# Group statistics of image 1 partly by a quadratic form: the last four chunks are multiplied out after the statistics are known

## Chip, cores and metric

The kernel runs on one core of a Trainium2 chip. The metric is the time of one execution on the device in microseconds; lower is better. The time before is the median of three runs.

## The reference

Two layers on x of shape (2, 1024, 64, 64), all in fp32. The first is a bottleneck with a deformable 3x3 convolution; its result x1 is the input of the second, a non-local block with a Taylor kernel and a normalisation over the whole image. What matters here is the end of the second:

```
t = einsum('oc,bchw->bohw', Wt, x1)          # and p, g alike, 512 channels
att_k = a_k^2 * sum(p**k * g)                # k = 0, 1, 2, over channels and pixels
y = att_0 + att_1 * t + att_2 * t**2
z = einsum('oc,bchw->bohw', Wz, y)           # 1024 channels
...
out = (z - mean(z)) / sqrt(var(z) + eps) * gn_w + gn_b + x1
```

Mean and variance are taken over all 1024 x 4096 values of an image (`_L1_conv_ref` has one group).

## The kernel before

The order of work on each engine is written out by hand, with semaphores between engines. An image is cut in 8 chunks of 512 pixels, 16 in all (`ALLC`). First the deformable convolution, x1 and the projections t, p, g are made chunk by chunk; x1 and t go to DRAM, the sums of p and g become three coefficients per image (`coefficients`).

Then comes the part that the change is about, a loop over 16 chunks with 8 output tiles each (`KIN` = 8; a tile is 128 channels x 512 pixels), 128 tiles in all, 64 (`ZT`) per image. Images, chunks and tiles are counted from 0: chunk 11 has tiles 88 to 95. For a chunk:

- POOL issues the load of t into `TB` (1 MB), once the low parts of the chunk before it are made.
- y is made in place in four parts (`KCP`): ACT scales (`y_scale`, L907, to two buffers `UB`), DVE multiplies (`y_square`, L1324), ACT rounds to the high part (`y_high`, L919), DVE takes the rest as the low part (`y_low`, L1328). y of chunk c + 1 is made between the tiles of chunk c.
- PE multiplies each tile with Wz in three passes (high x high, high x low, low x high; `product`, L194 to L196), 12 matmuls of 512 columns per tile. The first two and the last two tiles of a chunk are done together (`z_pair`). Six PSUM banks (`ZB`) take turns.
- ACT evicts the tile to one of 71 SBUF buffers (`z_evict`, L972) and DVE takes its statistics (`stats`, L1371). From tile 71 on an eviction waits until the store of the tile 71 before has landed.

When the 64 tiles of an image are in SBUF, the statistics are put together over partitions with two small matmuls (L1622, L1626), and each tile is finished: DVE adds x1 to the scaled tile (`add_x1`, L1406), ACT adds the bias (`fin`, L980), SP stores it. For image 0 this lies between the tiles of image 1, by a rule that says how many adds are through after x tiles of image 1:

```
def adds_by(x):
    return max(0, min(64, max(x - 3, 3 * (x - 5) // 2)))
```

x1 for it comes through four buffers (`XS`, 256 KB each): on SP a load, which waits for the add that frees its buffer, and a store, which waits for its bias pass, take turns. For image 1 it lies behind the last product. Its x1 comes in pairs of tiles (512 KB) into `XT`, slots in memory that is free by then.

## Time and profile before

| | |
|---|---|
| median of 3 runs | 2363.9 us (2363.74 to 2366.23) |
| profiled execution, its own time | 2355.59 us |
| its span | 2353.8 us |
| busy: PE, DVE, ACT, POOL | 2243.0, 1572.7, 1252.0, 778.6 us |
| DMA moved | 667.97 MB, mean 284 GB/s |

The profile is of one execution. Its span runs from the first to the last instruction that it records; the execution's own time is a little longer. PE is the matrix engine (PEld its weight loads), DVE the vector engine, ACT the scalar engine, POOL is GpSimd, SP only issues DMAs. "idle before us <-releaser" says how long an engine stood before an instruction and what ended this. A busy share is an average; here what matters is the last fifth of the span.

### The profile page before, as it was taken

What the parts mean: (1) busy time and instruction counts of PE and PEld (TensorE: products, weight loads), DVE (VectorE), ACT (ScalarE), POOL (GpSimd) and SP (SyncE); (2) the same over time, 40 slices, a digit from 0 to 9 for tenths busy, and PEclk for the clock granted to TensorE, in tenths of its full rate; (3) what the DMA queues carried; (4) which work ended last, traced back from release to release, by engine and by line L of the source; (5) the groups of instructions that cost most, each with busy time, mean ns of one, the idle gap of its engine ahead of it and who ended that gap; (6) DMA issues with size and microseconds to landing.
All of it is one profiled execution on the core that took longest, in us unless ns stands there. A gap on an engine that the chain in (4) does not pass through costs nothing.

```text
span 2353.8 us, 29804 instructions
## 1 busy us (share of the span) xinstructions
PE 2243.0 (95%) x10252; PEld 1853.8 (79%) x10252; DVE 1572.7 (67%) x3177; ACT 1252.0 (53%) x2432; POOL 778.6 (33%) x706
## 2 busy tenths in 40 slices
PE   8999999999989999999999999999999999999970
PEld 6888888888868788888878888788788878887750
DVE  4212325766788898889878988789785324557855
ACT  6444444444465666556655665565553324446745
POOL 0100003333224565556556765666561000000000
PEclk9999999999989999999999999999999999999985
DMA  8988989999998998889889988898884111118979
GB/s 304 320 310 279 314 291 381 403 400 394 401 375 286 315 341 308 297 320 336 288 294 315 314 313 307 295 313 305 289 305 156 60 49 53 54 50 288 314 229 388
DMA packets 289824, 667.97 MB, mean 284 GB/s; under 512 B 27112, under 2 KB 101608, under 8 KB 283528
## 3 DMA queue, kind: packets, MB, share of 16 engines
q0 software_dynamic: 88048, 322.81, 39.4%
q1 hardware_dynamic: 172536, 262.59, 31.4%
q10 hardware_dynamic: 29088, 80.67, 9.4%
q8 instruction: 81, 1.33, 0.2%
q14 instruction: 71, 0.58, 0.1%
HBM read 435.47 MB, written 230.49 MB: 283 GB/s over the span
## 4 chain that ended last, share of the span: by engine, by line
PE 86%; DMA 5%; DVE 5%; SPq 1%; issue 1%; ACT 1%; POOL 0%; ACTq 0%; DVEq 0%
PE bank L194 22%; PE bank L196 22%; PE bank L195 22%; PE bank L1462 5%; PE bank L1463 5%; PE bank L1464 5%; DVE z L1406 2%; PE bank L1480 2%; DMA xs<-x 2%; DMA g<-vwide,tbl 1%; DMA out<-z 1%; PE bank L1488 1%; PE bank L1504 1%; DMA xt<-x 0%; DVE zst L1371 0%
## 5 line engine op out<-in xcount | busy, mean ns | idle before, releaser
L647 POOL DMA_INDIRECT g<-vwide,tbl x512 | 589.9, 1152 | 548.9 <-DVE a L1018 208.1
L194 PE MATMUL bank<-x1h,wlh 128*128 128x512 f32 x1536 | 604.2, 393 | 5.4 <-DVE x1l L1296 3.9
L196 PE MATMUL bank<-x1h,wll 128*128 128x512 f32 x1536 | 601.6, 392 | 2.5 <-issue 2.5
L195 PE MATMUL bank<-x1l,wlh 128*128 128x512 f32 x1536 | 600.6, 391 | 2.8 <-issue 2.7
L1034 DVE SCALAR_TENSOR_TENSOR a<-g,tbl,a 128x256 f32<-128x256 f32 x1224 | 528.8, 479 | 23.7 <-DMA g<-vwide,tbl 18.4
L674 ACT ACTIVATE g<-g,tbl 128x256 f32<-128x256 f32 x1008 | 426.4, 499 | 200.2 <-DMA g<-vwide,tbl 158.1
L194 PEld LDWEIGHTS bank<-x1h,wlh 128*128 128x128 f32 x1536 | 289.4, 188 | 66.5 <-issue 6.1
L196 PEld LDWEIGHTS bank<-x1h,wll 128*128 128x128 f32 x1536 | 289.1, 188 | 66.8 <-issue 4.6
L195 PEld LDWEIGHTS bank<-x1l,wlh 128*128 128x128 f32 x1536 | 289.6, 189 | 66.0 <-issue 5.4
L752 ACT ACTIVATE vb<-bank 128x512 f32<-128x512 f32 (+1 forms) x320 | 174.3, 554 | 195.3 <-PE bank L1464 150.7
L1462 PE MATMUL bank<-w2h,o1h 128*128 128x512 f32 (+1 forms) x640 | 236.7, 370 | 0.0
L1463 PE MATMUL bank<-w2l,o1h 128*128 128x512 f32 (+1 forms) x640 | 235.8, 368 | 0.0
L1464 PE MATMUL bank<-w2h,o1l 128*128 128x512 f32 (+1 forms) x640 | 235.4, 368 | 0.0
L1089 DVE TENSOR_TENSOR xl<-xin,xh 128x1024 fp32r<-128x1024 f32 x64 | 78.2, 1225 | 222.6 <-ACT xh L724 222.5
L194 PE MATMUL bank<-yh,wzh 128*128 128x512 f32 x512 | 203.3, 397 | 5.0 <-DVE yl L1328 3.8
L196 PE MATMUL bank<-yh,wzl 128*128 128x512 f32 x512 | 202.0, 395 | 0.0
L195 PE MATMUL bank<-yl,wzh 128*128 128x512 f32 x512 | 201.6, 394 | 0.0
L651 POOL DMA_INDIRECT g<-vone,tbl x128 | 153.0, 1195 | 124.1 <-DVE a L1018 92.4
L662 POOL DMA_DIRECT2D tb<-t x16 | 8.7, 544 | 448.3 <-DVE yl L1328 436.8
L1371 DVE BATCH_NORM_STATS2 zst<-z 128x6 f32<-128x512 f32 x128 | 87.4, 690 | 104.0 <-ACT z L972 103.8
L1015 DVE TENSOR_TENSOR a<-a,g 128x512 f32<-128x512 f32 x224 | 153.4, 685 | 2.4 <-ACT g L674 1.7
L1018 DVE TENSOR_TENSOR a<-a,g 128x512 f32<-128x512 f32 x224 | 153.5, 685 | 0.0
(154 smaller groups left out, 3204.1 us busy)
## 6 DMA issues: line engine op xcount, KB each, us to landing
vwide<-vb SPq DMA_DIRECT2D x256, 256.0 KB, 4.3
vwide<-vb SPq DMA_DIRECT2D x112, 512.0 KB, 4.2
xf<-in_x SPq DMA_DIRECT2D x32, 1024.0 KB
x<-xf ACTq DMA_DIRECT2D x32, 1024.0 KB, 6.8
out<-z SPq DMA_DIRECT2D x128, 256.0 KB, 5.2
xin<-in_x ACTq DMA_DIRECT2D x54, 512.0 KB
t<-ts ACTq DMA_DIRECT2D x64, 256.0 KB
tb<-t POOLq DMA_DIRECT2D x16, 1024.0 KB, 5.4
```

The source lines that it names most:

```text
L194: nc.tensor.matmul(out, wh, xh, start=first, stop=False)
L195: nc.tensor.matmul(out, wh, xl, start=False, stop=False)
L196: return nc.tensor.matmul(out, wl, xh, start=False, stop=last)
L647: pool.indirect_dma_start(slot[:].rearrange("p a c -> p (a c)"), None, d["vwide"][img], bass.IndirectOffsetOnAxis(ap=at[:, i, tap(u), 0:1] ...
L674: ins = nc.scalar.activation(slot[:, c, :], slot[:, c, :], ACT.Copy, scale=TBL[p % 3][:, 1, tap(u), w:w + 1])
L752: nc.scalar.activation(VB[g % NVB][:, 0:n, a, :], RING[count % 4][:, 0:n * CMID].rearrange("p (t c) -> p t c", c=CMID), ACT.Copy).then_inc ...
L1015: nc.vector.tensor_tensor(acc, acc, slot[:, 0:2 * CMID], ALU.add).then_inc(half_done, 1)
L1018: nc.vector.tensor_tensor(acc, acc, slot[:, 2 * CMID:4 * CMID], ALU.add).then_inc(g_used[1], 1)
L1034: ins = nc.vector.scalar_tensor_tensor(out=acc, in0=slot[:, c, :], scalar=scale, in1=acc, op0=ALU.mult, op1=ALU.add)
L1462: nc.tensor.matmul(out, oh, W2H[:, k, lo:hi], start=k == 0, stop=False)
L1463: nc.tensor.matmul(out, oh, W2L[:, k, lo:hi], start=False, stop=False)
L1464: last = nc.tensor.matmul(out, ol, W2H[:, k, lo:hi], start=False, stop=k == KMID - 1)
```

## The change

For four of the 16 chunks the statistics no longer come from z. With y a pixel's 512 values, the sum of z^2 over channels is y'My with M = Wz'Wz, and the sum of z is the sum of y times the row sums of Wz. So:

- `DIRECT` = 96. The first 96 tiles go as before. At tile 88 (`M_AT`) PE makes M in 8 pieces (`piece`), from Wz in another layout (`wn`, 2 MB, buffers `RAW`), whose high and low parts ACT and DVE make piece by piece (`piece_high`, `piece_low`); the part of M below the diagonal comes from 6 transposes (`mirror`), and M too is split in high and low parts.
- Before tile 96 four `quadratic` chunks (12 to 15) run: for each, 32 matmuls of 512 columns give M x high part of y, and DVE multiplies that with 2y - high(y) and sums (`q_sum`). Then the statistics of image 1 are ready (`fin_mean_1`, `fin_var_1`, one small matmul).
- Then y of chunks 12 to 15 is made a second time, and tiles 96 to 127 are multiplied. These are not evicted: DVE adds x1 to the scaled tile from PSUM, to one of 12 buffers (`DIRECTS`). Two held tiles of image 1 (64 to 95) are finished with every two new ones, and stored, while PE goes on.
- POOL multiplies instead of DVE for y of chunks 9 to 11 and of the four quadratic ones (`q_square`).
- Adds of image 0 come denser (`added_by`): 35 instead of 27 before tile 88, 10 within M, 16 in chunk 11, 3 in the quadratic part. `fin` of an add is one event behind.
- On SP the loads of `XS` are put three stores ahead. x1 of image 1 has 14 slots as before, in other places: two can be loaded before image 0's stores are through, six after them, one more once the quadratic part runs, five after it.
- The row sums of Wz (`WBAR`, 8 DVE sums) are made where Wz is split, and each image has six coefficients instead of three.

The core of the diff:

```diff
+QUADS_Z = 4
+FIRST_Q = ALLC - QUADS_Z
+HELD = (CHUNKS - QUADS_Z) * KIN
+DIRECT = ZT + HELD
+MPIECES = KIN
+M_AT = DIRECT - KIN
...
+def added_by():
+    cum = []
+    for i in range(ZT, M_AT):
+        x = i - ZT
+        cum.append(11 * (x - 4) // 6 + 1 if x > 3 else 0)
+    for p in range(MPIECES):
+        cum.append(cum[-1] + 1 + (p % 4 == 3))
+    for i in range(KIN):
+        cum.append(cum[-1] + 2)
+    for k in range(KCP * QUADS_Z):
+        cum.append(cum[-1] + 1)
+    return [min(ZT, n) for n in cum]
...
-            for i in range(ZT):
+            for i in range(ZT + 3):
                 if i + len(XS) < ZT:
                     load_xs(i + len(XS))
-                store_out(i)
+                if i >= 3:
+                    store_out(i - 3)
...
+            for yc in range(FIRST_Q):
+                load_t(yc)
+                if yc == FIRST_Q - 1:
+                    for r, (lo, hi) in enumerate(RAW_RUNS):
+                        for tile in ((20, 21, 22, 23), (17, 18, 19), (24,))[r]:
+                            out_of(tile)
+                        pool.dma_start(RAW[r][:], d["wn"][:, lo:hi]).then_inc(raw_in[r], 16)
+                if yc > CHUNKS:
+                    for k in range(KCP):
+                        q_square(yc, k)
...
+            def piece(p):
+                pe.wait_ge(wl_done, WPIECES + p + 1)
+                high, low = MPH[p % 2], MPL[p % 2]
+                for k in range(KCP):
...
+                    rows, cols = slice(128 * k, 128 * k + 128), slice(128 * k, 128 * KCP)
+                    last = product(nc, ZB[k][:, 0:128 * (KCP - k)], high[:, rows], low[:, rows], high[:, cols], low[:, cols], p == 0, p == MPIECES - 1)
+                last.then_inc(mm_done, 1)
...
+            def quadratic(qi):
...
+                for k in range(KCP):
+                    pe.wait_ge(yh_done, KCP * yc + k + 1)
+                    for o in range(KCP):
+                        nc.tensor.matmul(q_bank(qi, o)[:], MH[k][:, 128 * o:128 * o + 128], YH[:, k, :], start=k == 0, stop=False)
+                        last = nc.tensor.matmul(q_bank(qi, o)[:], ML[k][:, 128 * o:128 * o + 128], YH[:, k, :], start=False, stop=k == KCP - 1)
+                    last.then_inc(q_done, 1)
...
+            for qi in range(QUADS_Z):
+                yc = FIRST_Q + qi
+                for k in range(KCP):
+                    y_square(yc + 1, k)
+                for k in range(KCP):
+                    adds(E_Q + KCP * qi + k)
+                for o in range(KCP):
+                    q_sum(qi, o)
+                for k in range(KCP):
+                    y_low(yc + 1, k)
+            fin_mean_1()
+            fin_var_1()
+            fin_scale(1)
```

Where the instructions stand now, at three places. In the rows the number behind a name is that of its buffer (and, after the underscore, of its tensor); L numbers are the lines of the kernel that the row is of. On POOL, before, after the last gather there are only the loads of t:

```order
L662 DMA tb_178<-t1 128x2048 [waits yl_done,t_out]
L662 DMA tb_178<-t2 128x2048 [waits yl_done,t_out]
L662 DMA tb_178<-t3 128x2048 [waits yl_done,t_out]
```

Now, from the load of t of chunk 11 to that of chunk 12:

```order
L765 DMA tb_184<-t11 128x2048 [waits yl_done,t_out]
L778 DMA raw0_273<-in_wn 128x2048 [waits out_done6,out_done7,out_done5,out_done4]
L778 DMA raw1_274<-in_wn 128x1536 [waits out_done3,out_done2,out_done1]
L778 DMA raw2_275<-in_wn 128x512 [waits out_done0]
L769 TENSOR_TENSOR tb_184<-ub0_187,tb_184 128x512 [waits u_done]
L769 TENSOR_TENSOR tb_184<-ub1_188,tb_184 128x512 [waits u_done]
L769 TENSOR_TENSOR tb_184<-ub0_187,tb_184 128x512 [waits u_done]
L769 TENSOR_TENSOR tb_184<-ub1_188,tb_184 128x512 [waits u_done]
L765 DMA tb_184<-t12 128x2048 [waits yl_done,t_out]
```

The squares of y stand on POOL now, and those of chunk 11 behind the three weight loads, which wait for stores of image 0 (`out_done`). And from the squares of chunk 13 to those of chunk 14:

```order
L769 TENSOR_TENSOR tb2_289<-ub1_188,tb2_289 128x512 [waits u_done]
L765 DMA tb2_289<-t15 128x2048 [waits yl_done,t_out]
L769 TENSOR_TENSOR tb_184<-ub0_187,tb_184 128x512 [waits u_done]
```

The load of t of chunk 15 waits for the low parts of chunk 13, and the squares of chunk 14 stand behind it.

On ACT, the evictions of tiles 83 to 85 (buffers z12 to z14) before:

```order
L972 ACTIVATE z12_195<-bank6 128x512 [waits out_done4,z_done]
L907 ACTIVATE ub1_182<-tb_178,coef1_80 128x512 [waits u2_done,coef_done,t_in]
L980 ACTIVATE z18_201<-z18_201,fb0_84 128x512 [waits sum_done]
L972 ACTIVATE z13_196<-bank2 128x512 [waits out_done5,z_done]
L907 ACTIVATE ub0_181<-tb_178,coef1_80 128x512 [waits u2_done,coef_done,t_in]
L980 ACTIVATE z19_202<-z19_202,fb0_84 128x512 [waits sum_done]
L980 ACTIVATE z20_203<-z20_203,fb0_84 128x512 [waits sum_done]
L972 ACTIVATE z14_197<-bank3 128x512 [waits out_done6,z_done]
```

and now, on to the first piece of the weights (`mph0`):

```order
L1113 ACTIVATE z12_201<-bank6 128x512 [waits out_done4,z_done]
L1038 ACTIVATE ub1_188<-tb_184,coef1_86 128x512 [waits u2_done,coef_done,t_in]
L1127 ACTIVATE z24_213<-z24_213,fb0_90 128x512 [waits sum_done]
L1127 ACTIVATE z25_214<-z25_214,fb0_90 128x512 [waits sum_done]
L1113 ACTIVATE z13_202<-bank2 128x512 [waits out_done5,z_done]
L1038 ACTIVATE ub0_187<-tb_184,coef1_86 128x512 [waits u2_done,coef_done,t_in]
L1127 ACTIVATE z26_215<-z26_215,fb0_90 128x512 [waits sum_done]
...
L1127 ACTIVATE z33_222<-z33_222,fb0_90 128x512 [waits sum_done]
L1145 ACTIVATE mph0_276<-raw0_273 128x512 [waits out_done1,raw_in0]
```

The bias passes are six tiles further along here (tile 24 where 18 was), and the third scaling (`ub0`, behind the eviction of tile 84) waits through `u2_done` for a square on POOL.

On SP, a load and the stores beside it, before:

```order
L553 DMA xs3_177<-x1_2 128x512 [waits sum_done]
L564 DMA out<-z15_198 128x512 [waits out_done7,o_done]
L553 DMA xs0_174<-x1_2 128x512 [waits sum_done]
L564 DMA out<-z16_199 128x512 [waits out_done0,o_done]
```

and now:

```order
L641 DMA xs3_183<-x1_2 128x512 [waits sum_done]
L654 DMA out<-z12_201 128x512 [waits out_done4,o_done]
L641 DMA xs0_180<-x1_2 128x512 [waits sum_done]
L654 DMA out<-z13_202 128x512 [waits out_done5,o_done]
```

The same load stands before the store of tile 12 instead of 15.

## Rows read from the trace of the kernel before

**Rows 1.** Page, the span in 40 slices, busy tenths: PE and DMA.
```profile
PE   8999999999989999999999999999999999999970
DMA  8988989999998998889889988898884111118979
```

**Rows 2.** Timeline of PE from 2270 on: start us, us, engine, line, operation.
```profile
2278.22 0.39 PE L196 MATMUL bank<-yh,wzl 128*128 128x512 f32 x1
```

**Rows 3.** Windows: us, busy of PE, PEld, DVE, ACT, POOL (x count), clock, DMA share, GB/s.
```profile
2164.00:2187.00 23.00, 22.25 (x96) 17.65 (x94) 17.65 (x29) 16.88 (x29) 0.54 (x1) 1.00 0.92 316
2300.00:2354.00 54.00, 0.00 (x0) 0.00 (x0) 27.95 (x42) 28.56 (x43) 0.00 (x0) 0.50 0.98 385
```

**Rows 4.** Timeline of POOL: the loads of t for image 0.
```profile
2007.46 0.54 POOL L662 DMA_DIRECT2D tb<-t  x1 [21.79 <-DVE yl L1328]
2029.78 0.54 POOL L662 DMA_DIRECT2D tb<-t  x1 [21.78 <-DVE yl L1328]
```

**Rows 5.** Timeline of PE, first matmuls of chunks 11 and 12.
```profile
2163.69 0.47 PE L194 MATMUL bank<-yh,wzh 128*128 128x512 f32 x1 [0.85 <-DVE yl L1328]
...
2187.06 0.47 PE L194 MATMUL bank<-yh,wzh 128*128 128x512 f32 x1 [0.81 <-DVE yl L1328]
```

**Rows 6.** Tile xs, 2050 to 2300: ns min/median/max, starts; waits; landings.
```profile
L1406 DVE SCALAR_TENSOR_TENSOR z<-z,fa,xs x64: 730/747/753, 2108.9 to 2238.7; 128x512 f32<-128x512 f32 x64
L553 SPq DMA_DIRECT2D xs<-x x60: 319/431/1087, 2109.7 to 2235.2; - x60
...
  DMA xs<-x: 21.6, 13
...
DMA to landing us min/median/max: 2.7/4.4/8.6
```

**Rows 7.** Tile z, 2050 to 2300: the stores and their landings.
```profile
L564 SPq DMA_DIRECT2D out<-z x78: 332/338/942, 2113.8 to 2298.9; - x78
...
DMA to landing us min/median/max: 2.0/4.8/8.5
```

**Rows 8.** Groups by shape from 1750 on: busy us, mean ns, idle before.
```profile
L980 ACT ACTIVATE z<-z,fb 128x512 f32<-128x512 f32 x128 | 87.1, 719 | 10.7 <-DVE z L1406 10.5
L907 ACT ACTIVATE ub<-tb,coef 128x512 f32<-128x512 f32 x64 | 51.4, 807 | 7.5 <-DMA tb<-t 7.3
L1324 DVE TENSOR_TENSOR tb<-ub,tb 128x512 f32<-128x512 f32 x64 | 44.0, 687 | 6.5 <-ACT ub L907 6.3
L651 POOL DMA_INDIRECT g<-vone,tbl x8 | 9.7, 1209 | 12.1 <-DVE a L1018 10.2 <-issue 1.8
L1304 DVE CUSTOM_DVE_ANT_0 gs<-bank,gs,sums 128x512 f32<-128x512 f32 x10 | 7.5, 747 | 32.8 <-PE bank L196 30.5 <-issue 2.3
L881 ACT ACTIVATION_READ_ACCUMULATOR gs<-bank 128x1 f32 x9 | 1.8, 197 | 0.0
L1304 DVE DVE_READ_ACCUMULATOR2_ANT sums<- 128x1 f32 x10 | 0.8, 83 | 0.0
```

**Rows 9.** Timeline of PE at 622 and 629: eight transposes; matmuls of 256 columns.
```profile
621.98 1.03 PE L1504 MATMUL bank<-ident,acl 128*128 128x128 f32 x8
...
629.43 0.28 PE L1463 MATMUL bank<-w2l,o1h 128*128 128x256 f32 x1
629.55 0.28 PE L1464 MATMUL bank<-w2h,o1l 128*128 128x256 f32 x1
```

**Rows 10.** Timeline of ACT: an eviction that waits for a store; two bias passes; tile 83's eviction.
```profile
2128.13 0.60 ACT L972 ACTIVATE z<-bank 128x512 f32<-128x512 f32 x1 [4.60 <-DMA out<-z]
...
2135.42 1.32 ACT L980 ACTIVATE z<-z,fb 128x512 f32<-128x512 f32 x2
...
2153.78 0.58 ACT L972 ACTIVATE z<-bank 128x512 f32<-128x512 f32 x1
```

**Rows 11.** Timeline of PE at 701, and the window around it.
```profile
701.25 0.79 PE L194 MATMUL bank<-o2h,w3h 128*128 128x512 f32 x1 [5.86 <-DVE o2l L1183]
700.00:710.00 10.00, 8.75 (x30) 7.09 (x31) 9.96 (x20) 6.33 (x13) 4.71 (x4) 0.73 0.96 336
```

436 lines of the change are left out of this document (348 added, 88 removed).

## The prediction

> **What bounds the kernel now.** I read the page's slices first: PE is at 9 tenths nearly throughout and at 7, then 0, in the last two, while DMA is full there [rows 1]. So the kernel is PE-bound until the z products end, and then a DMA-bound tail follows. The timeline of PE gives the edge: the last z product starts at 2278.22 [rows 2]. The span is 2353.8, so the tail is 75.6 us; in it DMA runs at 0.98 and 385 GB/s [rows 3]: 64 stores and most of image 1's x1 loads (images and tiles count from 0), which cannot start before the statistics of all 64 tiles of image 1 are known.
>
> Second, what holds PE before that. A chunk of z (8 tiles, 96 matmuls) takes 22.33 us undisturbed (two t loads of image 0, one per chunk [rows 4]), so 2.79 us a tile and 0.2326 us a matmul. Chunk 11 starts at 2163.69, chunk 12 at 2187.06 [rows 5]: 23.37 us, since PE waits 0.8 us at each start for DVE, which is late: it also adds x1 to image 0, and waits for these loads, 21.6 us in all [rows 6]. DMA is at 0.92 and 316 GB/s there [rows 3].
>
> **The change, part by part.** The sum is made on the profiled run: span 2353.8, its own time 2355.59; the median of the runs shown is 2363.9, 8.3 above, and I carry the difference over to it unchanged.
>
> *Tail.* Tiles 96 to 127 are multiplied after the statistics are known, and two held tiles go out with each two new ones. After the last product come two adds (0.75 each) [rows 6], one bias pass of 0.72 [rows 8], one issue 0.34 and a landing at 4.8 [rows 7], 7.3 us, the handovers against the overlap of neighbours on one engine. 75.6 becomes 7.3: **-68.3**. It needs that DMA keeps up: a pair of z products (5.6 us) brings 4 stores and 4 tiles of x1, 2.1 MB, or 377 GB/s, plus a t load a chunk. The tail moved 385 [rows 3], and 14 pairs of x1 are fetched ahead, so only the first nine pairs of z ask for that much. I cost it at nothing.
>
> *PE's new work.* The product of the weights with themselves has 24 matmuls each of 512, 384, 256 and 128 columns. A 512 is 0.2326, a 256 follows its predecessor by 0.12, eight 128-column transposes take 1.03, so 0.11 each [rows 9]. With 0.175 in between for 384: 24 x (0.233 + 0.175 + 0.12 + 0.11) = 15.3 us. No row has a 128-column matmul of this type; the ceiling is the 512's 0.233, +3 us. Six transposes: 0.7. The quadratic form: 128 matmuls of 512, 29.8. Together **+45.8**.
>
> *The way into the weight product.* The piece of order on POOL shows it: the three weight loads stand ahead of the squares of y chunk 11 and wait for the stores of tiles 20 to 24. ACT's third scaling of y (tile 84's place) needs the first of those squares. Before, tile 83 was evicted at 2153.78 to 2154.4 [rows 10]. From there: a scaling 0.72 and the pass over tile 24, 0.72, to 2155.9 (SP's store also follows the load that add 27 frees, done by then), issue 0.34, landing 4.8 [rows 7], POOL's issue 0.54 [rows 4], one square. A square on POOL is in no row: DVE does it in 0.69, and POOL's longest own operation took 1.21 [rows 8], so 0.69 to 1.2; I take 1.0, nearer the second since it is POOL's. That is 2162.6. The Trainium skill (GPSIMD Engine Reference, Elementwise — side-by-side cycle accounting) has the two-input operation at 1.96 times DVE's, by estimate 1.35 us here; by it the sum would be 1 to 2 us longer, over the places where squares are waited for. ACT then still has, in order, 2 scalings, 8 bias passes, 4 roundings, 3 evictions and the first weight piece (a pair of passes takes 1.32 [rows 10], so 0.6 from start to start, 0.7 for a scaling, 0.5 for an eviction), and DVE one subtraction: 11.9 us, so PE gets its first piece at 2174.5. PE, which runs up to six banks ahead, has finished tile 87 at about 2163.4, where chunk 11 starts now [rows 5]. **+11.1**, from 6 (landing at 2.0, ACT catching up) to 18 (landing at 8.5 [rows 7], tile 83 itself 3 late).
>
> *Inside the weight product.* Two buffers; PE needs 1.9 us a piece. ACT's copy 0.6 and DVE's subtraction 0.7 fit, with one or two adds, and the adds can come every 1.45 us: 0.75 + 0.43 + landing 4.4 + 0.2, over four xs buffers [rows 6]. Ten adds are 14.5 us against 15.3. Overrun **+1** (0 to 4). After PE had sat idle for 5.86 us, the 10 us around the restart had a mean granted clock of 0.73, so part of them at the lower level, 1.2 GHz, and 30 matmuls where the 8.75 us of work would hold 38 [rows 11]: some 1.9 us lost; here the restart is paced by ACT and DVE too: **+1**.
>
> *Chunk 11* carries 16 adds, 23.2 us at 1.45, what it takes now: **0** (-1 to +5). ACT has 16 bias passes, 8 evictions, 8 operations on y and 10 on the product, 23 us. Chunks 12 to 14 lose their adds: now 1 us late each at first, **-2.3** together.
>
> *Between the quadratic chunks.* The order on POOL puts the squares of chunk 14 behind a t load that waits for chunk 13's low parts, and these stand on DVE behind the four reductions of chunk 12's form. From the end of form 12: reductions 4 x 0.83, lows 4 x 0.75, issue 0.54, two squares 2.0, a scaling 0.8, a rounding 0.7 = 10.4, less the 7.4 of form 13 on PE: 3.0 idle. The same chain keeps pace with form 15, and each rounding now ends in an accumulator read of 0.20 [rows 8], partly covered, 0.6: **+3.6** (0 to 8).
>
> *From the form to z again.* Four reductions 3.3 and one low part 0.75 with handovers: **+4.3**. Then PE waits for the sums after its first pair (5.6 us): three lows, an aggregate and nine small operations: **+0.7**. The scale is there 3 us later and needed only six tiles on. POOL's other moves, the weight row sums and three more coefficients lie in stretches where DVE is idle half the time, and cost nothing.
>
> *x1 loads three stores ahead.* A load no longer stands behind the pass over the add just made; worth something only together with the denser adds (35 instead of 27 before tile 88), and it is what allows 1.45 above. **0**.
>
> Sum: -68.3 + 45.8 + 11.1 + 1 + 1 + 0 - 2.3 + 3.6 + 4.3 + 0.7 = -3.1. Median 2363.9 - 3.1 = **2361**.
>
> **Rivals.** *Stalls shorter.* If the store of tile 24 lands in 2.0, as some did [rows 7], and ACT absorbs the delay, PE waits 4 us for its first piece, and the quadratic chunks follow each other without a gap: -7.1 - 3.6, 2350; with a clean chunk 11 and no overrun (-1.1 - 1 - 1) 2347. For it: ACT is busy 17 of 23 us in such a chunk [rows 3]. Against: POOL's wait stands in the order.
>
> *x1 starves the adds (slower).* 61 adds have to be through by the end of chunk 11. In before 64 took from 2108.9 to 2238.7, 2.03 each, though 1.5 a tile were due, one in 1.86; DVE waited for xs 13 times. Landings rise to 8.6 [rows 6], and the weights add 2 MB in the same place: 32 MB of x1 and stores and 7 MB besides, from 2109 to 2204 where my sum without stalls has the end of chunk 11, is 410 GB/s, above the 385 of the tail [rows 3]. At 1.75 an add the way to the quadratic form takes 12 to 16 us more than my sum: 2374. ACT and DVE take their work in order, so a late x1 tile holds the eviction and, at the weight product, PE at once. It decides from about 1.6 us an add. For it: evictions waited 4.6 us for a store even at the old rate [rows 10].
>
> *POOL and DVE block each other (slower).* 28 squares move to POOL. If a square and an add can't run together, DVE loses up to 4 x 1.2 us a chunk; its 17.7 of 23 [rows 3] less the four squares and with the denser adds is 17, so 22 of 22.3: no room to catch up, and in chunk 11, 25: +6 to +10, 2368. No row of before can show it, since POOL computes nothing there. The Trainium skill (SBUF — State Buffer, SBUF: two separate sides) says exactly this of a DVE operation with two SBUF inputs and a GpSimd one that reads SBUF: the second is blocked until the first ends. By that rule this rival holds wherever the two meet, and the adds have two such inputs.
>
> *The tail does not go.* If stores can't run beside the products, image 1's 17 MB stay behind, at 385 GB/s 44 us: 2397. Against it: stores and products run together in every chunk of rows 3.
>
> **Numbers.** Forecast 0.45, its own range 2350 to 2370; short stalls 0.24; starved adds 0.20; POOL against DVE 0.08; the tail 0.03. A difference within 0.2% (2359.2 to 2368.6) is about what a measurement here can't tell from none. Of the forecast's 0.45, 0.20 lies below it, 0.16 within, 0.09 above. Faster: 0.20 + 0.24 = 0.44. Same: 0.16 and 0.03 of the port rival, 0.19. Slower: 0.09 + 0.20 + 0.05 + 0.03 = 0.37. The range, 2340 to 2382, takes in both larger cases up to their ends (shortest stalls with no overrun; starved adds with the port) and leaves 2 in 10 out.
>
> **What would show it.** Last PE product within 8 us of the end of the span; first weight piece 8 to 14 us after tile 87's product, with ACT's scaling waiting for POOL before it; pieces 1.9 to 2.2 apart; adds of image 0 every 1.45 to 1.6 us outside t loads; one gap of about 3 us before the third quadratic chunk, one of about 4 after the last. Wrong would be: a tail over 15 us, PE idle over 20 us around the weight product, adds at over 1.7 us, or squares over 1.5 us on POOL.

## The result and the profile after

| | before | after |
|---|---|---|
| median, 21 runs each, same chip | 2362.1 us (2350.9 to 2375.4) | 2382.2 us (2363.6 to 2403.8) |
| ratio, 95% interval | | 1.0084 (1.0066 to 1.0101) |
| profiled execution, its own time | 2355.59 us | 2386.72 us |
| its span | 2353.8 us | 2384.5 us |
| t load of chunk 9 to the end of the span | 257.0 us | 271.2 us |

The kernel became slower by 0.84%; 2361 had been predicted, and 2382.2 is just over the top of the range, 2382. The last row needs a word. The stages ahead of the z products are the same program in both kernels but for eight sums over Wz and some more coefficients, yet the two profiles differ there by 16.5 us. That is not the change: on one chip, runs with it (e1, e2, below) issue POOL's load of t for chunk 9 at 2080.91 and 2080.81, and one without it (e3) at 2080.80. This load comes before the first instruction of the z products that the change touches, so from it to the end of the span is the part that can be compared. I call it the **stage**. Timeline of POOL, that load, of before and then of after:

```profile
2096.77 0.54 POOL L662 DMA_DIRECT2D tb<-t  x1 [21.79 <-DVE yl L1328]
```

```profile
2113.26 0.53 POOL L765 DMA_DIRECT2D tb<-t  x1 [21.87 <-DVE yl L1553]
```

2353.8 - 2096.77 = 257.0, and 2384.5 - 2113.26 = 271.2: the stage is 14.2 us longer, where -3.1 was predicted. The miss is 17.3 us. (14.2 us of 2362 would be a ratio of 1.0060; the rest of 1.0084 lies ahead of the stage. The repetition below has 1.0065.)

The page's slices, PE and DMA, answer to [rows 1]; the last matmul of the timeline of PE answers to [rows 2]:

```profile
PE   7999999999989999999999999999999999996899
DMA  8998989999998999889888888798883211129978
```

```profile
2378.47 0.40 PE L249 MATMUL bank<-yh,wzl 128*128 128x512 f32 x1
```

The tail is gone: 2384.5 - 2378.47 = 6.0 us. PE is at 9 up to the end, but a 6 and an 8 stand where it was full before. The timeline of PE shows what they are (start us, us, operation; in brackets the idle time before it and what ended it), for the start of chunk 10, the first weight piece, the quadratic chunks 13, 14 and 15, and the first product after them:

```profile
2161.92 0.76 PE L247 MATMUL bank<-yh,wzh 128*128 128x512 f32 x1 [5.58 <-DVE yl L1553]
...
2200.74 0.80 PE L247 MATMUL bank<-mph 128*128 128x512 f32 x1 [13.46 <-DVE mpl L1603]
...
2252.48 0.47 PE L1977 MATMUL bank<-yh,mh 128*128 128x512 f32 x1 [3.70 <-ACT yh L1059]
...
2266.24 0.47 PE L1977 MATMUL bank<-yh,mh 128*128 128x512 f32 x1 [4.65 <-ACT yh L1059]
...
2275.78 0.47 PE L1977 MATMUL bank<-yh,mh 128*128 128x512 f32 x1 [0.41 <-ACT yh L1059]
...
2287.29 0.64 PE L247 MATMUL bank<-yh,wzh 128*128 128x512 f32 x1 [3.98 <-DVE yl L1553]
```

Windows (columns as in [rows 3]) show that PE also works more slowly behind each of these waits, since the granted clock is under 1 there (1.00 is 2.4 GHz; a mean below it has a part at 1.2 GHz):

```profile
2160.00:2180.00 20.00, 18.08 (x66) 14.47 (x67) 13.17 (x20) 14.63 (x25) 1.63 (x2) 0.83 0.93 323
2180.00:2200.00 20.00, 7.28 (x32) 5.51 (x30) 11.32 (x17) 10.93 (x19) 7.16 (x8) 0.80 0.90 309
2200.00:2220.00 20.00, 19.27 (x104) 17.71 (x105) 11.98 (x19) 11.38 (x21) 0.00 (x0) 0.86 0.98 353
2240.00:2260.00 20.00, 16.30 (x65) 13.02 (x64) 14.05 (x24) 15.52 (x29) 5.48 (x5) 0.91 0.93 317
2260.00:2280.00 20.00, 14.94 (x59) 11.58 (x58) 11.52 (x25) 11.97 (x24) 11.15 (x10) 0.91 0.89 334
2300.00:2360.00 60.00, 60.00 (x258) 48.23 (x258) 45.05 (x68) 44.28 (x69) 1.08 (x2) 1.00 0.98 373
```

What comes before the two largest waits stands on ACT, SP and POOL. ACT evicts tile 71 only when the store of tile 0 has landed. (The recorded expectations below call it tile 73 and the store of tile 2. Counted on ACT's timeline the wait of 8.97 is tile 71's: it is the second eviction behind the roundings of chunk 9, and the bias pass of tile 2 comes only after it.) In before this eviction, at 2119.22, did not wait; the longest wait for a store, 4.60 [rows 10], was tile 73's. The row of after:

```profile
2144.83 0.60 ACT L1113 ACTIVATE z<-bank 128x512 f32<-128x512 f32 x1 [8.97 <-DMA out<-z]
```

SP's timeline has the reason. The first store of all, tile 0's, goes out at 2137.26. Its tile had been finished since 2130.3 (ACT's first bias pass begins at 2129.57), but a load that waits for the fourth add stands ahead of it:

```profile
2128.82 8.40 SPq L641 DMA_DIRECT2D xs<-x  x3
2137.26 0.43 SPq L654 DMA_DIRECT2D out<-z  x1
2138.15 0.32 SPq L641 DMA_DIRECT2D xs<-x  x1
2138.52 0.74 SPq L654 DMA_DIRECT2D out<-z  x1
2139.30 0.45 SPq L641 DMA_DIRECT2D xs<-x  x1
2146.06 0.34 SPq L654 DMA_DIRECT2D out<-z  x1
```

POOL's timeline shows a square of chunk 10 that took 1.84 us; the weight loads, 21.17 us in wait for stores, and the squares of chunk 11 behind them; the load of t for chunk 13, right behind the squares of chunk 12; and the load of t for chunk 15, which waits for DVE with the squares of chunk 14 behind it:

```profile
2155.01 1.84 POOL L769 TENSOR_TENSOR tb<-ub,tb 128x512 f32<-128x512 f32 x1 [1.11 <-ACT ub L1038]
...
2186.06 1.60 POOL L778 DMA_DIRECT2D raw<-in_wn  x3 [21.17 <-DMA out<-z]
2187.68 3.71 POOL L769 TENSOR_TENSOR tb<-ub,tb 128x512 f32<-128x512 f32 x3
...
2238.56 0.59 POOL L765 DMA_DIRECT2D tb<-t  x1
...
2261.37 0.58 POOL L765 DMA_DIRECT2D tb<-t  x1 [8.22 <-DVE sq L1553]
2261.97 4.94 POOL L769 TENSOR_TENSOR tb<-ub,tb 128x512 f32<-128x512 f32 x4
```

ACT's third scaling of chunk 11 waits for the first of these squares:

```profile
2189.07 0.81 ACT L1038 ACTIVATE ub<-tb,coef 128x512 f32<-128x512 f32 x1 [9.56 <-POOL tb L769]
```

The tile xs (as [rows 6]) has a new thing in its first row, the maximum:

```profile
L1700 DVE SCALAR_TENSOR_TENSOR z<-z,fa,xs x64: 731/747/1741, 2125.8 to 2254.7; 128x512 f32<-128x512 f32 x64
...
  DMA xs<-x: 17.0, 15
...
DMA to landing us min/median/max: 2.6/4.8/8.7
```

An add took 0.75 before, always; now some take up to 1.74 us, beside a square on POOL. And 64 adds take (2254.7 - 2125.8) / 64 = 2.01 us each, no denser than the 2.03 of before, though the order asks for more. DVE waits for x1 17.0 us in all; it was 21.6 before [rows 6].

### The profile page after: what moved, and what is told of

Same layout as the page of the kernel before. It is cut to its first block, busy times and chain, and to the rows that moved or that the text cites. A ratio compares the mean times of both kernels' runs of the same rounds, so it can differ in the third digit from the quotient of the medians.

```text
span 2384.5 us, 30452 instructions
## 1 busy us (share of the span) xinstructions
PE 2306.0 (97%) x10480; PEld 1901.9 (80%) x10480; DVE 1588.5 (67%) x3219; ACT 1263.1 (53%) x2466; POOL 832.7 (35%) x741
## 4 chain that ended last, share of the span: by engine, by line
PE 89%; DMA 4%; issue 2%; DVE 2%; SPq 1%; ACT 1%; POOL 0%; ACTq 0%; DVEq 0%; POOLq 0%
PE bank L247 23%; PE bank L248 23%; PE bank L249 23%; PE bank L1788 5%; PE bank L1789 5%; PE bank L1790 5%; PE bank L1806 2%; DMA xs<-x 1%; DMA g<-vwide,tbl 1%; DMA xin<-in_x 1%; DMA out<-z 1%; PE bank L1814 1%; PE bank L1830 1%; DMA vone<-vb 0%; DVE z L1700 0%
## 5 line engine op out<-in xcount | busy, mean ns | idle before, releaser
L740 POOL DMA_INDIRECT g<-vwide,tbl x512 | 601.6, 1175 | 559.3 <-DVE a L1228 219.3
L247 PE MATMUL bank<-yh,wzh 128*128 128x512 f32 x512 | 204.8, 400 | 10.7 <-DVE yl L1553 9.6
L248 PE MATMUL bank<-yl,wzh 128*128 128x512 f32 x512 | 206.4, 403 | 0.0
L1511 DVE TENSOR_TENSOR x1l<-xf,x1h 128x512 fp32r<-128x512 f32 x128 | 84.0, 689 | 93.5 <-ACT x1h L1001 75.6
```

Of the source, the lines that this page charges most:

```text
L247: nc.tensor.matmul(out, wh, xh, start=first, stop=False)
L248: nc.tensor.matmul(out, wh, xl, start=False, stop=False)
L740: pool.indirect_dma_start(slot[:].rearrange("p a c -> p (a c)"), None, d["vwide"][img], bass.IndirectOffsetOnAxis(ap=at[:, i, tap(u), 0:1] ...
```

## Experiments

There are sixteen runs; e5 repeats the changed kernel and e14 repeats e10. The stage is the span less the issue of the t load of chunk 9, in the one profiled execution; the columns on waits are PE's, in us, and "-" is no wait that the timeline shows. "Gaps" are the waits before the quadratic chunks 13, 14 and 15 and the products after them, added up; in e10, e12, e14 and e15 they are one wait, before chunk 14.

A stage is one measurement. The two of e10 and e14, one kernel, differ by 2.6 us, those of after and e5 by 0.6. In ten of the sixteen runs the stage less 257.3 agrees to within 1.7 us with how far the run's median lies from before's on the same chip; the median says 2.2 us less in e6, and 2.5 to 5.5 more in e1, e4, e9, e10 and e14. So a difference of under 3 us between two stages is a hint and no more.

| run | t load | span | stage | chunk 10 | first piece | later pieces | gaps | ratio to before (95%) |
|---|---|---|---|---|---|---|---|---|
| before | 2096.77 | 2353.8 | 257.0 | 0.57 | | | | |
| after | 2113.26 | 2384.5 | 271.2 | 5.58 | 13.46 | - | 12.7 | 1.0084 |
| e1 | 2080.91 | 2350.2 | 269.3 | 5.68 | 8.39 | 2.55 | 12.1 | 1.0063 (1.0047 to 1.0080) |
| e2 | 2080.81 | 2354.9 | 274.1 | 3.98 | 15.90 | - | 14.2 | 1.0074 (1.0057 to 1.0091) |
| e3 | 2080.80 | 2338.1 | 257.3 | 0.17 | | | | 1.0002 (0.9993 to 1.0012) |
| e4 | 2081.82 | 2352.4 | 270.6 | 5.73 | 3.05 | - | 12.8 | 1.0062 (1.0045 to 1.0079) |
| e5 | 2081.00 | 2352.8 | 271.8 | 5.57 | 14.35 | - | 12.6 | 1.0065 (1.0048 to 1.0082) |
| e6 | 2080.26 | 2346.9 | 266.6 | - | 15.92 | - | 13.2 | 1.0034 (1.0023 to 1.0046) |
| e7 | 2083.79 | 2349.0 | 265.2 | 5.74 | 12.80 | - | 6.8 | 1.0030 (1.0017 to 1.0042) |
| e8 | 2081.69 | 2351.2 | 269.5 | 5.75 | 9.46 | 0.63 | 12.9 | 1.0055 (1.0039 to 1.0072) |
| e9 | 2099.85 | 2353.5 | 253.7 | - | 13.29 | - | 6.3 | 1.0013 (0.9989 to 1.0036) |
| e10 | 2110.90 | 2361.1 | 250.2 | - | 10.43 | 0.69 | 3.8 | 0.9978 (0.9954 to 1.0002) |
| e11 | 2106.77 | 2379.5 | 272.7 | 5.49 | 8.58 | 1.74 | 12.7 | 1.0066 (1.0039 to 1.0092) |
| e12 | 2080.86 | 2342.1 | 261.2 | - | 12.13 | 2.59 | 12.9 | 1.0012 (1.0003 to 1.0021) |
| e13 | 2082.45 | 2336.9 | 254.5 | 0.74 | 7.80 | - | 11.1 | 0.9989 (0.9980 to 0.9998) |
| e14 | 2082.11 | 2329.7 | 247.6 | - | 10.50 | - | 3.4 | 0.9980 (0.9971 to 0.9989) |
| e15 | 2080.32 | 2337.8 | 257.5 | - | 10.85 | 0.84 | 10.0 | 0.9994 (0.9985 to 1.0003) |
| e16 | 2079.99 | 2330.8 | 250.8 | 0.26 | 4.18 | - | 11.2 | 0.9970 (0.9958 to 0.9982) |

### e1_weights_after

POOL: the three weight loads behind the squares of chunk 11.

```diff
                 load_t(yc)
-                if yc == FIRST_Q - 1:
-                    for r, (lo, hi) in enumerate(RAW_RUNS):
...
                 if yc > CHUNKS:
                     for k in range(KCP):
                         q_square(yc, k)
+                if yc == FIRST_Q - 1:
+                    for r, (lo, hi) in enumerate(RAW_RUNS):
...
```

> The changed kernel with the three weight loads behind the squares of y chunk 11 on POOL. In the changed kernel ACT's third scaling waits 9.6 us for POOL, and PE 13.5 us for the first weight piece. Theory (POOL's queue is the cause): ACT's wait for POOL goes, but the weights are issued only when the stores of tiles 20 to 24 have landed all the same and need some 7 to 9 us to land, so the wait moves from ACT's scaling to the first piece: PE's wait 8 to 13 us, the z stage (from the load of t of chunk 9 to the end of the span, 271 us in the changed kernel) 267 to 272. Rival (the queue only hid a backlog of adds and passes): PE's wait stays at 13 us and more, the stage at 271 or over.

The wait before the first piece is 8.39, and 2.55 come up at a later piece; with the repetition e5 as base (14.35) that is 3.4 us less, and 2.5 less in the stage. ACT's waits for POOL's squares fall from 16.8 in after to 7.1. So the order on POOL is part of the wait; most of it stays. The ratio, 1.0063 for 1.0065, shows no gain.

### e2_loads_not_ahead

SP as before: load, store, in turns.

```diff
-            for i in range(ZT + 3):
+            for i in range(ZT):
                 if i + len(XS) < ZT:
                     load_xs(i + len(XS))
-                if i >= 3:
-                    store_out(i - 3)
+                store_out(i)
```

> The changed kernel with load and store of a tile in the old order on SP. Theory (x1 loads ahead are what lets the adds come denser): more waits of DVE for xs than the 17.0 us of the changed kernel, 25 us or more, and the stage 3 to 8 us longer than 271. Rival (the loads ahead push the first stores back by three tiles, and tile 73's eviction, which waited 9.0 us for one, pays for it): this eviction waits 4 to 5 us as before the change, PE's wait of 5.6 us at chunk 10 goes, and the stage is 3 to 6 us shorter.

DVE waits 28.1 us for x1 (18 times), as the theory said, and the stage is 2.3 longer than e5, less than its 3 to 8. The longest wait of an eviction for a store is 4.0 instead of 9.0, as the rival said, but PE still waits 3.98 us at chunk 10. Counted from the t load, chunk 10 starts at 47.1 here, at 48.6 in e5, at 43.5 before. So the loads ahead cost its start 1.6 of the 5.1 us, and the rest comes with the old order too: between 2094 and 2128 DVE waits 7.2 us for x1, where e5 has 1.4 in the like stretch, and ACT's passes and evictions are late behind it.

### e3_layout_alone

The kernel before with the change's new small buffers and its further input, nothing else.

```diff
+    WBAR, YSUM = m.put("wbar", [128, KIN, KCP]), m.put("ysum", [128, 4, KCP])
+    WK, YK, QS, TS1 = (m.put(n, [128, KCP]) for n in ("wk", "yk", "qs", "ts1"))
...
+    wn = per_part(g["L1_conv_Wz"].reshape(CIN, CP))
```

> The kernel before, with nothing of the change but its memory: the second copy of Wz as an input that nobody reads, and the new small buffers, so that everything behind them in SBUF and DRAM lies where the change has it. In the profiled runs the load of t of chunk 9 was issued at 2096.8 before and at 2113.3 after, though no instruction ahead of it was changed except in the last projection chunk. Theory (chance: runs of one kernel differ by this much): time within 0.2% of the kernel before. Rival (the placement slows the gathers): 5 to 15 us slower than before.

Ratio 1.0002, stage 257.3. Nothing of the loss is placement, and 257.3 can stand for the stage of before on that chip.

### e4_pe_kept_busy

48 matmuls of 512 columns, whose result nobody reads, ahead of the first weight piece.

```diff
                 if KIN * zc == M_AT:
+                    for n in range(48):
+                        nc.tensor.matmul(PT[:], WZH[:, 0, 0, :], WZH[:, 0].rearrange("p k c -> p (k c)"), start=True, stop=True)
```

> The changed kernel with 48 matmuls of 512 columns into a free bank before the first weight piece, 11.2 us, inside PE's wait of 13.5 us. In the changed kernel the clock is at 0.80 to 0.86 in the 40 us around this wait. Theory (the idle time costs the clock, and the clock some us): granted clock 0.95 or more from 2180 to 2220, first three pieces 1.9 apart instead of 2.4 and more, the stage 2 to 3 us shorter than 271. Rival (the first pieces are paced by ACT and DVE anyway): clock higher, stage the same within 1 us.

PE waits 3.05 us instead of 14.35. In the first 10 us from the first piece the granted clock is 0.83; in e5, where PE had idled 14.35, it is 0.72. Windows of e4, then of e5:

```profile
2169.00:2179.00 10.00, 9.58 (x50) 8.86 (x51) 6.85 (x11) 5.84 (x11) 0.00 (x0) 0.83 1.00 379
```

```profile
2168.00:2178.00 10.00, 9.98 (x45) 9.14 (x46) 5.86 (x10) 4.89 (x9) 0.00 (x0) 0.72 1.00 377
```

50 matmuls against 45. Over the 40 us from 2148 the clock is 0.96, and 0.79 in e5 from 2147, as the theory said; but the first pieces are 3.4 and 2.0 us apart, not 1.9, and the stage is only 1.2 us shorter, near the rival. The ratios don't tell the two kernels apart. So nothing here speaks against the prediction's price for the clock behind this wait (+1); the wait itself is the matter.

### e5_changed_again

> The changed kernel itself, unchanged, beside the next three on one chip, so that they have a measured base. From POOL's issue of the t load of chunk 9 to the end of the span it took 271.2 us in its profile, against 257.0 in the kernel before. Theory (the loss lies in three places of the z stage: chunk 10, the way into the weight product, the quadratic chunks): 270 to 272 again, and a ratio to before of 1.006 to 1.009, as the placement of memory alone cost nothing. Rival (part of the loss came from the stages ahead, where the two first profiles differed by 16 us): the ratio on this chip is far from that, under 1.004 or over 1.010, while the stretch from the t load stays 271.

Stage 271.8, ratio 1.0065, as the theory said. It is the base of the next three, on the same chip.

### e6_first_stores

```diff
-        cum.append(11 * (x - 4) // 6 + 1 if x > 3 else 0)
+        cum.append(max(11 * (x - 4) // 6 + 1, min(2 * (x - 3), x if x > 5 else 4)) if x > 3 else 0)
...
+            loaded = len(XS)
+            for i in range(ZT):
+                ahead = min(ZT, i + len(XS) + 1 + min(3, max(0, i - 3)))
+                for j in range(loaded, ahead):
+                    load_xs(j)
+                loaded = ahead
+                store_out(i)
```

and ACT finishes the adds of the first two events at once, not one event later. So three things change together: when the first adds come, when their passes come, and how far the loads run ahead.

> The first adds of image 0 come two at a time (four before the low parts of chunk 9 are made), ACT finishes them at once, and SP lets the loads run ahead only from the fourth store on, so the store of tile 2 goes out some 8 us earlier. Theory A (chunk 10 starts 5.6 us late because the eviction of tile 73 waits 9 us for the store of tile 2, which stands behind the load that add 3 frees): that wait falls under 1 us, PE's wait before chunk 10 under 1.5, and the stage from 271 to 263 to 266. Rival B (x1 comes too slowly for the denser adds): the waits only move, to a later eviction or to xs; PE idles 3 us or more somewhere before tile 88, and the stage stays 269 or more.

No eviction waits for a store any more, PE doesn't wait at chunk 10, and 5.2 us go from the stage (266.6, just outside the 263 to 266 of theory A). Which of the three changes does it was not separated; by e2 the loads ahead alone account for 1.6 us. Windows of e5 and e6 over the same stretch of chunk 10:

```profile
2126.00:2146.00 20.00, 16.36 (x64) 13.18 (x65) 14.21 (x21) 15.27 (x27) 2.82 (x3) 0.91 0.93 325
```

```profile
2126.00:2146.00 20.00, 19.82 (x85) 15.59 (x84) 12.45 (x20) 10.14 (x17) 0.16 (x1) 1.00 0.97 335
```

21 matmuls more in 20 us: PE is busy 3.5 us longer, and the clock is 1.00 instead of 0.91. But the wait before the weight product grew by 1.6. Counted from the t load, PE comes to this wait 7.1 us earlier than in e5 (65.6 for 72.7), and the first piece only 5.5 (81.5 for 87.0): ACT and DVE, who make it, had not gained as much.

### e7_quadratic_order

A third t buffer and a second buffer for the weights of the sums (in place of tiles 48 to 55, whose stores are through), and the order of three queues:

```diff
             load_t(FIRST_Q)
+            load_t(FIRST_Q + 1)
             for yc in range(FIRST_Q, ALLC):
                 for k in range(KCP):
                     q_square(yc, k)
-                if yc == FIRST_Q:
-                    load_t(yc + 1)
                 load_t(yc + 2)
...
+                for k in range(KCP):
+                    y_low(yc + 1, k)
                 for o in range(KCP):
                     q_sum(qi, o)
-                for k in range(KCP):
-                    y_low(yc + 1, k)
```

> Only the quadratic part: t of chunk 13 is loaded ahead of the squares of chunk 12, a third t buffer takes chunk 14 (in place of tiles 48 to 51), the weights of the sums have two buffers, DVE makes the low parts of the next chunk before it sums the form of this one, ACT's roundings go between its scalings. Theory A (the gaps there, 3.7, 4.7, 0.4 and 4.0 us, come from the order of loads and passes, and the lower clock behind each gap goes with them): the four gaps fall under 2 us together, and the stage from 271 to 257 to 261 (12.7 of gaps and up to 3 of clock, less 2). Rival B (ACT, POOL and DVE together can't prepare a chunk in the 7.5 us of a form): each gap stays 1.5 us or more, form starts 9 us apart, and the stage is 266 or more.

The stage is 265.2: between the two theories, near the rival's bound. The gaps fell from 12.6 to 6.8; a new wait of 1.7 for the sums came up behind them. A form now can be prepared in the time of the one before but for some 2 us.

### e8_pieces_early

```diff
+                if yc == FIRST_Q - 1:
+                    load_raw(0)
                 if yc > CHUNKS:
                     for k in range(KCP):
                         q_square(yc, k)
+                        if yc == FIRST_Q - 1 and k % 2:
+                            load_raw(1 + k // 2)
...
+                if i == M_AT - 1:
+                    piece_high(0)
                 z_evict(i)
+                if i == M_AT - 1:
+                    piece_high(1)
```

> Only the way into the weight product: the three weight loads stand between the squares of chunk 11, each where its tiles' stores have landed, instead of all ahead of them, and the first two weight pieces are made before and right after the eviction of tile 87. Theory A (the 13.5 us before the first piece are one chain: store of tile 24, loads, squares, scalings, passes, first piece): the wait before the first piece falls to 0 to 3 us, and the stage from 271 to 260 to 264 (the weight product itself then runs at 1.9 us a piece and full clock). Rival B (ACT and DVE are late for their own work there, whatever POOL does, as the 8.4 us suggest that stayed when only the order on POOL was changed): 6 us or more stay before the first piece or come up inside the product, and the stage is 267 or more.

Here the rival holds: 9.46 stay, stage 269.5. With e1 (8.39 and 2.55) it says that some 9 us of this wait stay when no square stands behind the weight loads.

### e9_three_together

e6, e7 and e8 in one kernel.

> The edits of the three runs before in one kernel: first stores early, quadratic order, pieces early. Alone they gave, from the t load of chunk 9 to the end, 266.6, 265.2 and 269.5 us against the changed kernel's 271.8. Theory A (three separate places, each loss its own): the gains add up, 5.2 + 6.6 + 2.3 = 14.1, stage 257 to 259, time within 3 us of before (whose stage is 257.3), ratio 0.998 to 1.002. Rival B (one shared limit behind all, such as DMA or the ports, that shows elsewhere once a place is mended): at least 4 us of the 14.1 don't arrive, stage 262 or more, ratio over 1.002.

The stage is 253.7: 18.1 less, even more than 14.1 and outside both theories. Counted from the t load to the first product behind the forms, the gains just add up: e6, e7 and e8 reach it 6.5, 8.6 and 3.6 us sooner than e5, 18.7 together, and e9 18.6. Behind it e6, e7 and e8 give back 1.3 to 2.0 us each, e9 0.5; why is open. The run's chip scattered much (before: 2343 to 2366), and the ratio doesn't follow: 253.7 against 257.3 would be 0.9985, just below its interval, 0.9989 to 1.0036. So e9 is shown to be about as fast as before, not faster.

### e10_three_and_order, and e14_three_and_order_again

e9, and: only the first weight load ahead of the squares; two squares of chunk 13 ahead of the third buffer's load; the squares of chunk 12's second y on POOL; two scalings of chunk 13 ahead of the roundings of chunk 12, and the last bias passes of chunk 11 behind those of chunk 13; the sums one tile later on PE.

```diff
                         q_square(yc, k)
-                        if yc == FIRST_Q - 1 and k % 2:
-                            load_raw(1 + k // 2)
+                if yc == FIRST_Q - 1:
+                    load_raw(1)
+                    load_raw(2)
...
+            q_square(FIRST_Q + 1, 0)
+            q_square(FIRST_Q + 1, 1)
+            load_t(FIRST_Q + 2)
```

> As the run before, and: only the first weight load stands ahead of the squares of chunk 11 (the second one waited 5.8 us there for a store with two squares behind it); two squares of chunk 13 ahead of the third t buffer's load, which waited 5.3 us for a store; POOL also squares chunk 12 for its products; the bias passes of the last two adds of chunk 11 behind the roundings of chunk 13; the sums one tile later. Theory A (each remaining wait of PE there, 9.5 before the weight product, 1.8, 2.7, 2.3 and 1.7 in and behind the quadratic part, is a matter of what stands ahead in a queue): 5 to 8 us less than the run before, stage 250 to 253, ratio 0.995 to 0.998, so faster than both kernels. Rival B (ACT and DVE are at their limit there): 2 us or less.

> The kernel with three places and orders mended once more, on another chip, since its first interval, 0.9954 to 1.0002, held 1. Its stage of 250.2 us against 257.3 of before says -7.1 us, 0.997; theory A: 0.996 to 0.998 with the interval below 1. Rival: the stage gain is given back ahead of it, ratio 0.999 or more with the stage still at 250.

Stage 250.2 and 247.6. On the quieter chip the ratio is 0.9980 (0.9971 to 0.9989): **faster than before by 0.2%**, and than the changed kernel by 0.8% (0.9980 / 1.0065, from two chips). The first run has 0.9978, but its interval holds 1. The profiled execution of e14 is the fastest of its eleven, so 247.6 flatters it; the median says 5.2 us less than before. Forms 12 and 13 now follow each other without a gap. This is the best version that I found.

### e11_squares_on_dve

All squares back on DVE.

```diff
             def y_square(yc, k):
-                if CHUNKS < yc < ALLC:
-                    return
...
             for yc in range(FIRST_Q, ALLC):
-                for k in range(KCP):
-                    q_square(yc, k)
```

> The changed kernel with the squares of chunks 9 to 11 and of the quadratic chunks on DVE, as in the kernel before; nothing else. Theory A (POOL's squares cost little by themselves; their harm is that they stand behind loads): adds of image 0 at 0.75 us each again instead of up to 1.74 beside a square, the wait before the weight product down from 14 to 9 to 11, since no square stands behind the weight loads, but up to 1 us more in a quadratic gap; stage 267 to 271. Rival C (POOL and DVE block each other, the 0.08 case of the prediction): stage 264 or less. Rival D (DVE has no room for them): PE waits 2 us or more longer in chunks 10 to 12 or at the quadratic gaps, stage 273 or more.

Tile xs of this run:

```profile
L1692 DVE SCALAR_TENSOR_TENSOR z<-z,fa,xs x64: 733/747/754, 2118.9 to 2245.6; 128x512 f32<-128x512 f32 x64
```

No add over 0.754 us: the stretched adds are POOL's doing. But the stage is 272.7, 0.9 more than e5. The wait before the weight product fell to 8.58 (and 1.74 later), so the first piece comes 4.9 us sooner; but from there to the first product behind the forms it takes 92.3 us for 87.6: PE waits 1.7 us more and needs 3.1 more for the same 326 matmuls, at a granted clock of 0.87 for 0.91. Rival C (stage 264 or less) falls, theory A misses its 267 to 271, and rival D's 273 is nearest, though the gaps it named did not grow (12.7). The run moves 28 squares to DVE and takes away the blocking and the queue on POOL at once; it shows only that these come out even, and doesn't price the blocking alone.

### e12_last_orders and e15_sums_first

Two trials to remove the wait of 3.4 to 3.8 us that e10 and e14 have before the third form. PE waits there for the sums of chunk 12, which stand on DVE behind five adds and four low parts:

```profile
2217.55 0.50 PE L2024 MATMUL bank<-yh,mh 128*128 128x512 f32 x1 [3.36 <-DVE qs L1668]
```

e12 puts the adds behind the low parts and sums (and moves the first weight load behind two squares); e15 has sums, low parts, adds in the first step, and lets SP run no loads ahead from store 50 on. The first step of the quadratic part on DVE in e15:

```diff
-                for k in range(KCP):
-                    adds(E_Q + KCP * qi + k)
+                if qi == 0:
+                    for o in range(KCP):
+                        q_sum(qi, o)
                 for k in range(KCP):
                     y_low(yc + 1, k)
...
+                for k in range(KCP):
+                    adds(E_Q + KCP * qi + k)
```

> As the kernel with three places and orders mended (stage 250.2 from the t load of chunk 9 to the end), and: the first weight load behind two squares of chunk 11 instead of ahead of all (ACT waited 2.5 us for a square there), and in the quadratic part the low parts and the sums ahead of the adds (PE waited 3.8 us for the sums of chunk 12, which stood behind five adds). Theory A (orders in queues): the 3.8 us before the third form go to under 1, the wait before the weight product from 10.4 to 8 to 9; stage 244 to 247, ratio 0.994 to 0.997. Rival B (DVE and ACT are full there): stage 249 or more.

> As the kernel with three places and orders mended (stage 247.6 and 250.2 in its two profiles, 3.4 to 3.8 us of PE's wait before the third form for sums that stand behind adds), and: in the first quadratic step DVE makes the sums of chunk 12 first, then the low parts of chunk 13, then the adds; from store 50 on SP no longer lets loads run ahead, so the stores of tiles 52 to 55, whose place the second buffer takes, go out earlier. The run before this one had moved the adds alone and got a wait of 12.9 us in that place, with DVE waiting 6.8 us for such a store. Theory A (orders in queues): no wait over 1 us before the third form, stage 244 to 247, ratio 0.9955 to 0.9975. Rival (low parts behind the sums come too late for the t load of chunk 15): a wait of 3 us or more moves to the fourth form, stage 248 or more.

Both fell. In e12 PE waits 12.86 us there, in e15 10.04. (The first weight load behind two squares didn't help either: 12.13 and 2.59 in e12, for 10.50.) The waits of e12, then of e15, in that stretch:

```profile
ACT z L1154 <- DVE z L1742: 10.7, 1, 10.7
DVE sq L1594 <- DMA out<-z: 6.8, 1, 6.8
```

```profile
DVE z L1742 <- DMA xs<-x: 8.3, 3, 5.2
ACT z L1154 <- DVE z L1742: 7.9, 2, 5.9
```

ACT's bias passes stand ahead of its scalings of chunk 14. Adds moved back on DVE hold ACT there, for 10.7 and 5.9 us, and with it the next chunk of y. I had looked at DVE's queue alone. In e15 the x1 loads, no longer ahead, came late as well.

### e13_no_x1_loads and e16_no_x1_loads_pieces_early

The changed kernel, and e8, without the x1 loads of image 0 from the fifth tile on; x1 of other tiles is then added to most of image 0.

```diff
-                at_least(sp, sum_done, i - len(XS) + 1)
-                sp.dma_start(XS[i % len(XS)][:], d["x1"][i // KIN][:, i % KIN, :]).then_inc(xs_in[i % len(XS)], 16)
+                if i < len(XS):
+                    sp.dma_start(XS[i % len(XS)][:], d["x1"][i // KIN][:, i % KIN, :]).then_inc(xs_in[i % len(XS)], 16)
```

> The changed kernel without the x1 loads of image 0 from the fifth tile on, and without the waits for them: the adds take what is in the four buffers, so x1 of other tiles is added to most of image 0. 15.7 MB less of DMA in chunks 8 to 12, and no add waits for x1. Rival 2 of the prediction (x1 starves the adds, and what is behind them on DVE and ACT): the wait before the weight product falls from 14 to under 7, the adds keep their order's pace, and the stage falls from 271 by 8 us or more. Theory A (the losses are orders in queues, x1 itself is not late by much): the eviction of tile 73 waits less, since its store no longer stands behind a load (stage -5 as in the run on the first stores), another 1 to 3 from the 15 us in which DVE waits for x1; wait before the weight product 10 or more; stage 263 to 266.

> The changed kernel without image 0's x1 loads from the fifth tile on (they and their waits are left out, as in the run before without them) and with the weight loads between the squares and the first two pieces made early. Alone the first left 7.8 us before the weight product, the second 9.5, from 14.4. Theory X (two separate causes meet there, the supply of x1 that makes ACT and DVE late, and the queue on POOL; the later one counts): together 0 to 4 us are left, stage 248 to 251. Rival (both shorten the same chain, and the rest is ACT's and DVE's own work on chunk 10): 6 us or more stay, stage 253 or more.

e13 takes 17.3 us from the stage, more than the whole loss, twice what rival 2 asked for and far outside theory A; 64 adds come in (2205.8 - 2095.0) / 64 = 1.73 us each. The first piece, e13 and then e16:

```profile
2156.71 0.79 PE L247 MATMUL bank<-mph 128*128 128x512 f32 x1 [7.80 <-DVE mpl L1603]
```

```profile
2150.14 0.79 PE L247 MATMUL bank<-mph 128*128 128x512 f32 x1 [4.18 <-DVE mpl L1612]
```

From 14.35: 9.46 with POOL's order mended, 7.80 without x1 loads, 4.18 with both. 4.18 is just over what theory X allowed, and the stage (250.8) is within it, but its picture of two chains of which the later counts doesn't hold: then taking away the shorter alone would bring nothing. PE's own arrival moves too, so the first piece is better counted from the t load. It comes at 87.0 us in e5, 83.4 in e8, 74.3 in e13 and 70.2 in e16: 3.6, 12.8 and 16.9 sooner. The two gains add up, as for two delays one behind the other on the way to this piece, and x1's is the larger: without its loads POOL waits 12.8 us for the stores of image 0 where e5 has 20.7.

About 5 of e13's 17.3 us are the start of chunk 10, which e6 mends as well. The other 12 are what x1's loads cost the changed kernel: adds that wait for it, and 15.7 MB in the way of stores, t and weights. The run takes both away and can't tell them apart. Nor is 12 a part of the loss of 14.2 as it stands, since the kernel before has the same loads and was not run without them. It can't owe them much, though: PE's waits from chunk 10 to 14 came to 3.8 us there.

## Why the prediction was wrong

PE's stage laid beside the prediction's terms; each length is from a row above or from the timeline of PE (chunk 11 starts at 2218.29, the first form at 2241.35):

| part | predicted | measured | miss |
|---|---|---|---|
| t load of chunk 9 to tile 87 | 66.6 | 74.0 | +7.4 |
| wait for the first piece | 11.1 | 13.5 | +2.4 |
| weight product | 17.3 | 17.6 | +0.3 |
| chunk 11, transposes | 24.1 | 23.1 | -1.0 |
| four forms and the gaps between | 33.4 | 42.0 | +8.6 |
| form to z | 4.3 | 4.0 | -0.3 |
| 32 tiles of z, wait for the sums | 89.8 | 91.2 | +1.4 |
| last product to the end | 7.3 | 6.0 | -1.3 |

The sum is 17.5, the miss of 17.3 but for rounding.

- **Tail, DMA in the last phase:** right. 75.6 became 6.0, and DMA ran at 0.98 and 373 GB/s beside full products.
- **PE's new work:** right. The weight product with overrun and clock took 17.6 for 17.3; pieces come 1.92 us apart once the clock is up (6 of them from 2206.77 to 2216.37), for 1.9.
- **The way into the weight product:** the named chain was there, the scaling behind the square behind the loads, 13.5 for 11.1, but the near hit is in part luck. Counted from the t load the first piece was due at 77.7 us and came at 87.5, 9.8 late; the wait is only 2.4 off because PE came 7.4 late too. ACT's part behind the first square was right, 11.8 for 11.9. What was late is the start: tile 83 is evicted 6.2 us later, the loads go out 6.2 us after the issue of tile 23's store where a landing was set at 4.8, and three weight loads take 1.6 us to issue where one with 0.54 was counted. The store of tile 24 goes out at 2182.20, 3.9 us after its bias pass, behind a load that waits for the 28th add, which the prediction took as done; this add itself waited 2.1 us for x1.
- **A square on POOL:** 1.29 us alone, for 1.0; outside the 0.69 to 1.2 that the rows gave. The estimate from the Trainium skill's page (GPSIMD Engine Reference, Elementwise — side-by-side cycle accounting), 1.35, was nearer; by that rule the trace agrees.
- **"x1 loads three stores ahead: 0":** this is the first step that failed, together with the adds "every 1.45 us" that the loads were to allow. The loads ahead help DVE (28.1 us of waits for x1 without them in e2, 15.6 with them in e5), but the first stores then stand behind loads: the eviction of tile 71, which did not wait before, waits 8.97, and chunk 10 starts 5.1 us later. No term looked at chunk 10 at all. With its clock it is the +7.4, and e6 takes it away. By e2 the order of the loads is 1.6 of the 5.1; with the old order the denser adds wait for x1 instead.
- **"Between the quadratic chunks +3.6":** the second that failed. The gap before chunk 14 was foreseen as 3.0 and came as 4.65. The one before chunk 13, 3.70, was not: POOL issues t of chunk 13 behind the squares of chunk 12, at 2238.56; it lands 8.7 us later, ACT waits 1.5 us for it, and four scalings and squares follow. 5.2 us of the miss are gaps, 3.4 the clock, which the term had at full: from 2240 to 2280 it was 0.91. e7 takes half of the gaps away by order alone, e14 all but 3.4.
- **The adds "every 1.45 us":** wrong; 2.01. DVE waited for x1 17.0 us in 15 waits of up to 4.1. The 1.45 came from a median landing; the longest was 8.7, and ACT and DVE pass each late tile on. The rows of before spoke against it: 2.03 where the order asked for 1.86 [rows 6]. Even without x1 loads (e13) an add takes 1.73.

Of the rivals, *x1 starves the adds* was nearest: 2.01 an add, over its bound of 1.6, and e13 shows that x1's loads hold up the changed kernel by some 12 us, beside the start of chunk 10. Its 2374 had no term for the quadratic chunks, where 8.6 of the 17.5 us lie. What share of the loss is x1's and what the orders', the runs don't settle: e14 mends it by orders and a few more buffers, with all the x1 loads in place. *POOL and DVE block each other* happens: an add up to 1.74 us, a square up to 1.84. The Trainium skill (SBUF — State Buffer, SBUF: two separate sides) says that of such a DVE and such a GpSimd operation the second has to wait for the first, and the trace agrees: 1.74 for 0.75, 1.84 for 1.29. But e11, with no square on POOL, is no faster, so the 7 us of this rival aren't there to be had by moving the squares back. *The tail does not go* fell.

The mechanism of the change was right: the tail went. The gain was given back in waits of the queues that feed PE, and the same change with other orders (e14) is faster than before by 0.2%.
